# The last stage of a graph network kernel as one pipeline over chunks of 512 rows

## What is computed

```python
# end of block 1: out holds the sum over the edges; H is the convolution's linear part
out = out + H * (dinv * dinv)[:, None]
x = x + relu(out)
# block 2
h = maximum(layernorm(x), 0)
agg = segment_sum(edge_attr, dst)            # 6250 x 128
model_in = concatenate([h, agg, u[0]])       # 384 wide
z1 = relu(model_in @ W1 + b1)
z2 = relu(z1 @ W2 + b2)
x = x + z2 @ W3 + b3
```

## Time and profile before

| | us | share of the span |
|---|---|---|
| median of three runs | 1022.87 | |
| profiled execution, its own time | 1022.51 | |
| its span | 1020.8 | |
| TensorE busy | 897.6 | 88% |
| VectorE busy | 596.3 | 58% |
| ScalarE busy | 527.0 | 52% |
| GpSimd busy | 602.7 | 59% |

### The profile page before, as it was taken

One profiled execution on the slowest core, in us unless ns is written; L12 is line 12 of the kernel. 1 busy time (PEld: TensorE's weight loads), 2 busy tenths in 40 slices (PEclk: granted clock), 3 DMA queues, 4 the chain that ended last, 5 costly groups with the idle time before them and its releaser, 6 DMA issues. The chain is left out here.

```text
span 1020.8 us, 23249 instructions
## 1 busy us (share of the span) xinstructions
PE 897.6 (88%) x9338; PEld 631.7 (62%) x9338; DVE 596.3 (58%) x1266; ACT 527.0 (52%) x949; POOL 602.7 (59%) x592
## 2 busy tenths in 40 slices
PE   1794243999999999999999999999999999997577
PEld 1673120577777777777777777777777777775245
DVE  5985774455555555555565555555555555552944
ACT  0482052555555555555555555555555555552685
POOL 2000215777777777777777777777777777742614
PEclk9986555899999999999999999999999999998989
DMA  6000044565666556655655666556655655643103
GB/s 183 11 2 1 2 126 155 176 193 175 200 204 204 177 180 201 201 178 182 201 183 173 201 202 198 167 189 203 201 166 193 201 173 184 202 135 100 43 22 105
DMA packets 83735, 158.04 MB, mean 155 GB/s; under 512 B 11558, under 2 KB 31332, under 8 KB 83628
## 3 DMA queue, kind: packets, MB, share of 16 engines
q1 hardware_dynamic: 66348, 121.11, 36.0%
q0 software_dynamic: 17280, 35.42, 12.6%
HBM read 150.08 MB, written 6.41 MB: 153 GB/s over the span
## 5 line engine op out<-in xcount | busy, mean ns | idle before, releaser
L812 POOL DMA_INDIRECT gathered<-scaled_h_table,index x540 | 546.8, 1013 | 206.3 <-issue 151.5
L824 ACT CAST counts_sb<-ps_counts 128x588 fp32r<-128x588 f32 x540 | 393.4, 729 | 365.4 <-PE ps_counts L982 361.9
L997 PE MATMUL ps_product<-table_sb,counts_sb 128*120 128x256 f32 x2646 | 486.2, 313 | 0.0
L997 PEld LDWEIGHTS ps_product<-table_sb,counts_sb 128*120 128x120 f32 x2646 | 387.1, 185 | 0.3 <-ACT counts_sb L824 0.3
L982 PE MATMUL ps_counts<-key_hot,lo_hot 128*128 128x294 bf16 x1080 | 310.4, 305 | 19.2 <-DVE key_hot L881 19.2
L876 DVE TENSOR_TENSOR lo_hot<-src_lo,iota_lo 128x512 bf16<-128x512 f16 x270 | 114.2, 423 | 182.9 <-PE ps_counts L982 180.0
L881 DVE TENSOR_TENSOR key_hot<-key,iota_key 128x1176 bf16<-128x1176 f16 x270 | 207.5, 768 | 0.0
L982 PEld LDWEIGHTS ps_counts<-key_hot,lo_hot 128*128 128x128 bf16 x1080 | 99.8, 101 | 122.6 <-issue 61.4
L1015 PE MATMUL ps_sums<-attr,attr_hot 128*32 128x128 f32 x2160 | 116.8, 289 | 3.5 <-DMA attr<-in_edge_attr_dram 3.5
L931 DVE TENSOR_TENSOR acc<-acc,ps_product 128x96 f32 (+1 forms) x135 | 37.1, 275 | 130.5 <-PE ps_product L1045 119.2
L1015 PEld LDWEIGHTS ps_sums<-attr,attr_hot 128*32 128x32 f32 x2160 | 42.9, 109 | 56.6 <-issue 34.6
(11 more groups left out here) (194 smaller groups left out, 706.3 us busy)
## 6 DMA issues: line engine op xcount, KB each, us to landing
attr<-in_edge_attr_dram SPq DMA_DIRECT2D x80, 1280.0 KB
gathered<-scaled_h_table,index POOLq DMA_INDIRECT x540
scaled_h_table<-row_ring SPq DMA_DIRECT2D x12, 256.0 KB, 2.3
xs<-in_x_dram SPq DMA_DIRECT2D x12, 256.0 KB, 5.2
out_dram<-y_ring SPq DMA_DIRECT2D x12, 256.0 KB, 2.3
attr<-in_edge_attr_dram SPq DMA_DIRECT2D x1, 640.0 KB
attr<-in_edge_attr_dram SPq DMA_DIRECT2D x2, 320.0 KB
raw_d<-in_dst_dram SPq DMA_DIRECT2D x1, 540.0 KB
```

The costliest lines, as they stand in the source:

```text
L812: pool.indirect_dma_start(gathered[:, n % GATHERS, g, :], None, table, bass.IndirectOffsetOnAxis(ap=index[:, s * CG + g, t:t + 1], axis=0) ...
L824: act.copy(counts_sb[d % 2][:, :, 2 * k * WT:(2 * k + 2) * WT] .rearrange("p h (t n) -> p t h n", n=WT), ps_counts[n % 2][:, :, 0:KEYS].re ...
L997: ins = pe.matmul(ps_product[d % 2][0:CP, 0:2 * P], counts_sb[d % 2][:, h, :], table_sb[:, h, :, :].rearrange("p a f -> p (a f)"), start=( ...
```

## The change

The two loops and the middle of the last stage become one loop. All chunks pass through all steps in it, and each engine's program is written as a few functions of a chunk, called at distances NORM to OUT of 1 to 6 rounds.

- The root, mean and variance are worked out for each chunk of four blocks: GpSimd does `variance(c)` in six operations on four columns, ScalarE the root, VectorE the reciprocal and the shift (`norm`).
- VectorE does the Relu with dinv in one scalar_tensor_tensor over the chunk, where ScalarE did it in four.
- The attribute product goes to the same PSUM group as the first layer's other product, in `layer_one`; the copy to `acc`, `sum_ring` and VectorE's add are gone. ScalarE reads the sum from PSUM.
- ScalarE copies the turned rows to SBUF, where VectorE did.
- `ps_1` and `ps_2` have one bank each instead of two; the convolution's transposes have two banks of their own, `ps_conv`.
- The loads of x for chunks 0 and 1 are issued ahead of the weights and b3, the others after them.

```diff
--- before.py
+++ after.py
@@ -1088,238 +1088,263 @@
...
-            M1_AT, SUM_AT, Z1_AT, M2_AT, Z2_AT, M3_AT, Y_AT = 1, 2, 2, 3, 4, 5, 6
+            def by_block(ap):
+                return ap.rearrange("p (b f) -> p b f", f=P)
+
+
+            NORM, TURN, ONE, TWO, THREE, OUT = 1, 2, 3, 4, 5, 6
...
-                    sp.dma_start(w1_sb[:], w1.rearrange("(k p) n -> p k n", p=P)).then_inc(w_in, 16)
-                    sp.dma_start(w2_sb[:], w2).then_inc(w_in, 16)
-                    sp.dma_start(w3_sb[:], w3).then_inc(w_in, 16)
                     for c in range(CHUNKS - 1):
-                        sp.dma_start(xs[:, c * BC:(c + 1) * BC, :], x_full[:, c * BC:(c + 1) * BC, :])\
-                          .then_inc(x_in[c], 16)
+                        sp.dma_start(xs[:, blocks(c), :], x_full[:, blocks(c), :]).then_inc(x_in[c], 16)
+                        if c == 1:
+                            sp.dma_start(w1_sb[:], w1.rearrange("(k p) n -> p k n", p=P)).then_inc(w_in, 16)
+                            sp.dma_start(w2_sb[:], w2).then_inc(w_in, 16)
+                            sp.dma_start(w3_sb[:], w3).then_inc(w_in, 16)
+                            sp.dma_start(b3_rows[:], b3.rearrange("(a n) -> a n", a=1).to_broadcast([P, P]))\
+                              .then_inc(b3_in, 16)
                     sp.wait_ge(zeroed, 1)
                     sp.dma_start(xs[0:TAILN, FB, :], x[FB * P:N, :]).then_inc(x_in[CHUNKS - 1], 16)
-                    sp.dma_start(b3_rows[:], b3.rearrange("(a n) -> a n", a=1).to_broadcast([P, P]))\
-                      .then_inc(b3_in, 16)
...
+                    def add_self(c):
+                        if c >= 2:
+                            pool.wait_ge(conv_ready, c - 1)
+                        parts = table_sb[:, blocks(c), :, :].bitcast(F32)
+                        pool.tensor_tensor(by_block(slot(self_ring, c)), parts[:, :, 0, :], parts[:, :, 1, :], ALU.add)\
+                            .then_inc(self_ready, 1)
+
+                    def variance(c):
+                        at = blocks(c)
+                        pool.wait_ge(stats_ready, c + 1)
+                        m0, m1, s0, s1 = (stats[:, at, k] for k in (1, 4, 2, 5))
+                        link(pool.tensor_tensor(spread[:, at], m0, m1, ALU.subtract))
+                        pool.tensor_tensor(mean[:, at], m0, m1, ALU.add)
+                        pool.tensor_tensor(var[:, at], s0, s1, ALU.add)
+                        link(pool.tensor_tensor(spread[:, at], spread[:, at], spread[:, at], ALU.mult))
+                        link(pool.tensor_scalar(spread[:, at], spread[:, at], P / 4.0, None, ALU.mult))
+                        pool.tensor_tensor(var[:, at], var[:, at], spread[:, at], ALU.add).then_inc(var_ready, 1)
+
+                    def add_bias(c):
+                        if c == 0:
+                            pool.wait_ge(b3_in, 16)
+                        if c >= 2:
+                            pool.wait_ge(y_ready, c - 1)
+                        pool.wait_ge(x1_ready, c + 1)
                         n = width(c)
-                        if c >= 2:
-                            pool.wait_ge(conv_ready, c - 1)
-                        parts = table_sb[:, c * BC:c * BC + n, :, :].bitcast(F32)
-                        pool.tensor_tensor(slot(self_ring, c).rearrange("p (b f) -> p b f", b=n), parts[:, :, 0, :],
-                                           parts[:, :, 1, :], ALU.add).then_inc(self_ready, 1)
-                    pool.wait_ge(b3_in, 16)
-                    pool.wait_ge(x1_ready, CHUNKS)
-                    for c in range(CHUNKS):
-
-                        n = width(c)
-                        if c >= 2:
-                            pool.wait_ge(y_ready, c - 1)
-                        pool.tensor_tensor(slot(x3_ring, c).rearrange("p (b f) -> p b f", b=n),
-                                           xs[:, c * BC:c * BC + n, :],
-                                           b3_rows[:].unsqueeze(1).to_broadcast([P, n, P]), ALU.add)\
-                            .then_inc(x3_ready, 1)
+                        pool.tensor_tensor(by_block(slot(x3_ring, c)), xs[:, blocks(c), :],
+                                           b3_rows[:].unsqueeze(1).to_broadcast([P, n, P]), ALU.add).then_inc(x3_ready, 1)
+
+                    add_self(0)
+                    for s in range(CHUNKS + THREE):
+                        if s + 1 < CHUNKS:
+                            add_self(s + 1)
+                        if s < CHUNKS:
+                            variance(s)
+                        if s >= THREE:
+                            add_bias(s - THREE)
...
                     def add_conv(c):
...
+                        n = width(c)
                         v.wait_ge(self_ready, c + 1)
                         v.wait_ge(conv_turned, c + 1)
...
+                        v.tensor_tensor(slot(conv_ring, c), ps_conv[c % 2][:, 0:n * P], slot(self_ring, c), ALU.add)\
+                         .then_inc(conv_ready, 1)
+                        v.wait_ge(conv_ready, c + 1)
+                        link(v.scalar_tensor_tensor(out=by_block(slot(relu_ring, c)), in0=by_block(slot(conv_ring, c)),
+                                                    scalar=0.0,
+                                                    in1=dinv[:, blocks(c)].unsqueeze(2).to_broadcast([P, n, P]),
+                                                    op0=ALU.max, op1=ALU.mult))
+                        v.wait_ge(x_in[c], 16)
+                        v.tensor_tensor(xs[:, blocks(c), :], by_block(slot(relu_ring, c)), xs[:, blocks(c), :], ALU.add)\
+                         .then_inc(x1_ready, 1)
+                        v.wait_ge(x1_ready, c + 1)
+                        for b in range(c * BC, c * BC + n):
+                            ins = v.bn_stats(stats[:, b, :], xs[:, b, :])
+                        ins.then_inc(stats_ready, 1)
+
+                    def norm(c):
+                        at = blocks(c)
+                        v.wait_ge(root_ready, c + 1)
+                        link(v.reciprocal(rstd[:, at], rstd[:, at]))
+                        v.scalar_tensor_tensor(out=shift[:, at], in0=mean[:, at], scalar=-0.5, in1=rstd[:, at],
+                                               op0=ALU.mult, op1=ALU.mult).then_inc(norm_ready, 1)
+
+                    def finish(c):
+                        v.wait_ge(m3_ready, c + 1)
+                        v.wait_ge(x3_ready, c + 1)
+                        if c >= 2:
+                            v.wait_ge(y_out[c % 2], 16 * (c // 2))
+                        v.tensor_tensor(slot(y_ring, c), ps_3[c % 2][:, 0:width(c) * P], slot(x3_ring, c), ALU.add)\
+                         .then_inc(y_ready, 1)
+
+                    for s in range(CHUNKS + OUT):
                         if s < CHUNKS:
...
+                            add_conv(s)
+                        if s == 0:
+                            v.wait_ge(b1u_ready, 1)
+                            v.tensor_tensor(b1u[:], ps_1[:, 0:1], B1, ALU.add).then_inc(b1u_done, 1)
+                        if NORM <= s < CHUNKS + NORM:
+                            norm(s - NORM)
+                        if s >= OUT:
+                            finish(s - OUT)
...
+                    def root(c):
+                        at = blocks(c)
+                        act.wait_ge(var_ready, c + 1)
+                        act.activation(rstd[:, at], var[:, at], ACT.Sqrt, bias=eps_col[:], scale=1.0 / P)\
+                           .then_inc(root_ready, 1)
+
+                    def normalize(c):
+                        act.wait_ge(norm_ready, c + 1)
+                        if c >= 2:
+                            act.wait_ge(h2_turned, c - 1)
                         for k in range(width(c)):
...
+                            n = c * BC + k
+                            ins = act.activation(h2_ring[:, c % 2, k * P:(k + 1) * P], xs[:, n, :], ACT.Relu,
+                                                 scale=rstd[:, n:n + 1], bias=shift[:, n:n + 1])
+                        ins.then_inc(h2_ready, 1)
+
+                    def save_turned(c):
+                        act.wait_ge(h2_turned, c + 1)
+                        if c >= 2:
+                            act.wait_ge(m1_ready, c - 1)
+                        act.copy(slot(h2t_ring, c), ps_turn[c % 2][:, 0:width(c) * P]).then_inc(h2t_ready, 1)
+
+                    def save_one(c):
+                        if c == 0:
+                            act.wait_ge(b1u_done, 1)
+                        act.wait_ge(m1_ready, c + 1)
+                        if c >= 2:
+                            act.wait_ge(m2_ready, c - 1)
+                        act.activation(slot(z1_ring, c), ps_1[:, 0:width(c) * P], ACT.Relu, bias=b1u[:])\
+                           .then_inc(z1_ready, 1)
+
+                    def save_two(c):
+                        act.wait_ge(m2_ready, c + 1)
+                        if c >= 2:
```

(89 more changed lines are left out.)

130 lines of the change are left out of this document (6 added, 124 removed).

## The result

The changed kernel takes 1036.74 us, the median of four runs (1034.91 to 1039.02), against 1023.08 us before, also of four runs. The ratio is 1.0137, with a 95% interval of 1.0114 to 1.0159: it is slower, by 1.4%. The profiled execution has 1036.35 us and a span of 1034.6.

What follows compares the result with a forecast made beforehand. A closed loop through TensorE, ScalarE and VectorE bounds each round: 6.36 us plus 0.4 waiting for GpSimd gives 6.76; entry to 960.0, nine rounds to 1020.8, and the end make span 1034.1, time 1036, range 1028 to 1047.

Steps and rivals of the forecast that it cites:

- a round without waits: Steady part of the merged loop: one closed round through TensorE, ScalarE and VectorE without GpSimd waits, 6.36 us.
- chunk 11: End of chunk 11's layer one, 4.7 us after chunk 10's because the one-block chunk 12 is normalised in that round: 1025.5.
- last y: End of the last adds, 2.7 us after chunk 12's layer one at 1028.5, ahead of the final store.
- The loop: Merged stage: save one, root, shift, normalise, h2 transposes, layer three and layer one close once a round, 6.36 us.
- Whatever the distance of the stages in chunks: Queue orders of TensorE and ScalarE: every round is one closed loop, however many chunks apart the stages stand.
- GpSimd's term: VectorE's shift waits for GpSimd's bias add each round: 0.4 us (bounds 0 and 1.27), pitch 6.76.
- The clock: Rival: TensorE's granted clock falls back to 0.50, 2.83 us more a round, 1049 to 1061 us; chance 0.07.
- The end: From chunk 10's layer one at 1020.8 to the end of the span at 1034.1.
- TensorE's busy share: Steady rounds: TensorE busy 4.35 of 6.76 us, 64%, with the granted clock expected at 1.00.
- The store at the end: Store of the last output after the last adds: 2.9 us, as in the kernel before.
- Entry and weights: Start of the stage: weights, behind two x loads, land at 939.0; TensorE stands at the u product until then.
- The rival of free engines: Merged loop: engines run freely and TensorE's own work sets the pitch, 4.35 us, time about 1014; chance of faster 0.08.

Runs made afterwards that it cites:

- e1: Changed kernel with the h2 transposes, the three layers and the output each one round later; 1022.12 us, ratio 0.9995 to the kernel before.
- e2: Changed kernel with layer one's attribute product made twice; 1046.46 us, ratio 1.0238 to the kernel before.
- e3: Changed kernel with layer two's product made twice; 1037.81 us, ratio 1.0154 to the kernel before.
- e8: Changed kernel without GpSimd's bias add, so b3 is missing in the output; 1034.98 us, ratio 1.0102 to the kernel before.
- e9: e1 with TensorE's and ScalarE's orders turned, and VectorE's conv add and Relu product kept in PSUM; 1009.71 us, ratio 0.9875 to the kernel before.
- e10: e1 with VectorE's conv add and Relu product written back to their PSUM bank; 1018.86 us, ratio 0.9963 to the kernel before.
- e11: Changed kernel with its distances kept and only TensorE's and ScalarE's orders within the round turned; 1045.89 us, ratio 1.0211 to the kernel before.
- e4: Changed kernel with GpSimd's bias add held back until the shift of chunk s is done; 1038.47 us, ratio 1.0148 to the kernel before.
- e7: Kernel before with only the attribute product moved into layer one's PSUM group, its copy and add gone; 1028.63 us, ratio 1.0052 to the unedited one.

## Why the prediction was right, and where it wasn't

The forecast was 1036 us, slower, and 1036.74 was measured. Step by step, against the marks that it had set:

| step | predicted | measured |
|---|---|---|
| end of layer one, chunk 0 | 954.4 | 954.2 |
| end of layer one, chunk 1 | 960.0 | 959.7 |
| a round without waits | 6.36 | 6.32 |
| shift's wait for GpSimd, mean over nine rounds | 0.4 | 0.17 |
| clock | no price | 1.6 in one round |
| end of layer one, chunk 10 | 1020.8 | 1019.7 |
| chunk 11 | 1025.5 | 1024.6 |
| last y | 1031.2 | 1030.9 |
| end of the span | 1034.1 | 1034.6 |

- **The loop** was right in its path and in its size: its terms are all in the chain of waits, and e1, e2 and e3 show that it is a matter of order.
- **"Whatever the distance of the stages in chunks" was wrong.** The loop is one round long because the h2 transposes of a chunk come exactly one round after its normalise. With one more round between the two (e1) it no longer binds. The step of the prediction that led there holds for the change as it is, but its general wording doesn't.
- **GpSimd's term was too large.** The mechanism is there. Of nine rounds four have it, with 0.23, 0.54, 0.56 and 0.18 us, 1.5 in all against 3.6 in my sum. The rest of the time GpSimd's adds passed the shift by or were about to end (one ends at 987.52, the shift of 987.44 takes 0.16). The six small operations took 0.20 to 0.24 us each when nothing was in their way, as estimated. The shift in a round where it waits, after:

```profile
966.85 0.29 ACT rstd L1242
...
967.38 0.72 DVE shift L1215
```

- **The clock** was a rival with 0.07, and it came true for one round. In the profile after, the granted clock is 0.84 and 0.81 in the two stretches from 1005 to 1015. In the chain of waits the h2 transposes from 1008.48 take 1.11 in place of 0.66, layer three 1.71 in place of 0.89 and the attribute product 1.20 in place of 0.86, and that round is 7.93 us in place of 6.32. Ahead of it TensorE had only one block of conv transposes left, and two gaps of 0.67 and 1.15 us. But e8 has the same round with the same two gaps, before 1009.18 and 1011.46, and its clock reads 1.00 all through, so they don't explain the fall. Its cause stays open.
- **The end** was too short by 1.6 us: from chunk 10's layer one to the end of the span 14.9, not 13.3. It and the 1.6 of the clock made up by luck for a GpSimd term that was 2.1 too large and nine plain rounds that were 0.4 too long together, so the total is closer than its terms.
- **TensorE's busy share** in the steady part is 73%, not 64%. The forecast divided the spacing of products by the round, while the view counts each instruction's whole length (1.02 us for the two matmuls of a product, with the next product 0.86 after its start).
- **The store at the end** took 3.7 us after the last y, not 2.9. That is half of what the end was short by.
- **Entry and weights** were right: the u product starts at 939.09, where 939.0 was taken.
- **The rival of free engines** was rightly set aside for this code. Its pitch of 4.35 isn't out of reach: e9 has it, by order, distance and place of the operands alone.

## What to carry to other kernels

When the programs of in-order engines are written as rounds, walk the waits from one round to the next and look for a path that comes back to the same engine after one round: its length is a floor for the pitch, however little each engine has to do, and one more round between two stages, or another order within the round once the distances are right, can remove it. Work added to such a loop costs its full length, while the same work at a place where the engine waits costs next to nothing. When the loop is gone, look at once for what is late next; here it was VectorE operations with two SBUF inputs beside GpSimd adds, and keeping an intermediate in PSUM removed that without an instruction more.

## What the runs showed of the hardware

- A VectorE operation on two SBUF tiles that starts under a GpSimd add waits for it (1.7 and 1.65 us for 0.69 in e1). The same operation with one input in PSUM takes 0.70 beside the same adds (e10). The wait goes both ways: GpSimd's self add of 1.26 shows 1.72 in e1. The Trainium skill says this too ("SBUF — State Buffer", Who interferes with whom). It says moreover that such a VectorE instruction contends with a GpSimd instruction that reads SBUF, not with one that only writes it. The trace of before has one such case, and it agrees: GpSimd clears a tile from 121.74 for 5.38 us (L589), and beside it VectorE's three one-column operations on two SBUF inputs (L627 to L629) take 0.16 each.
- A root of four columns takes 0.29 us, one of 49 takes 0.34, and thirteen changes between root and Relu brought no table load.
- The granted clock read 1.00 from 955 to 1005 in after, with TensorE idle 1.15 us in each round, 0.84 and 0.81 in the ten microseconds behind that, and 1.00 again from 1015 to 1020. It fell in e2 too (0.71 from 990 to 995), and for longer in e11 (0.83 from 960 to 1000), but not in the steady rounds of e3, e4 and e8. What decides was not tried.
- In the first loop of e7 TensorE has transposes alone, 1.11 us in every 2.10, and the granted clock reads 0.50 from 941 to 959. In the same loop of before, with an attribute product in each chunk, it reads 1.00 from 952 to 965.
